# Relative-shift transfers of an attention kernel: residual rows 36 partitions apart, 44 transfers a group in place of 32

## The reference, cut to what matters

```python
AC = einsum('bhid,bhjd->bhij', q + u_bias, k)
BD = einsum('bhid,hjd->bhij', q + v_bias, rp)     # rp: one row for each of 2L-1 distances
BD = _rel_shift(BD)                               # row i is moved left by an amount that depends on i
attn = softmax((AC + BD) * scale)
out = einsum('bhij,bhjd->bhid', attn, v)
```

## Time and profile before

| | |
|---|---|
| time, median of 3 runs | 3833.55 us (3824.93 to 3842.62) |
| time of the profiled execution | 3816.15 us |
| span of that execution | 3814.3 us |
| PE busy | 3139.2 us, 82% |
| ACT busy | 2553.6 us, 67% |
| DVE busy | 2489.7 us, 65% |
| POOL busy | 2399.5 us, 63% |
| granted clock of PE | 0.899 of full speed |

### The profile page before, as it was taken

The page is one execution under the profiler, slowest core; times in us unless marked ns, Lnnn a source line. Parts: engine busy times, 40 slices in busy tenths (PEclk is TensorE's granted clock), DMA queues, the critical chain, the costliest instruction groups (busy, mean ns, idle before and its releaser), DMA issues. The chain is left out here.

```text
span 3814.3 us, 115093 instructions
## 1 busy us (share of the span) xinstructions
PE 3139.2 (82%) x40768; PEld 2161.6 (57%) x40768; DVE 2489.7 (65%) x4784; ACT 2553.6 (67%) x3598; POOL 2399.5 (63%) x4232
## 2 busy tenths in 40 slices
PE   4564588889989888988888887888898989889955
PEld 2443266566656566655666665666665666656644
DVE  1544277677767666776767676776676767667845
ACT  2342477777777777776777776777777777777731
POOL 3234577677767666776777676766777667777700
PEclk7787599999999999998999998999999999999977
DMA  8224899898989898888898998988998888999731
GB/s 235 94 87 141 162 197 196 185 188 195 201 186 199 186 190 190 199 189 175 193 193 197 188 195 175 196 192 190 197 199 194 189 191 203 194 182 200 187 118 44
DMA packets 473330, 688.07 MB, mean 180 GB/s; under 512 B 296752, under 2 KB 394928, under 8 KB 404144
## 3 DMA queue, kind: packets, MB, share of 16 engines
q0 software_dynamic: 327680, 537.92, 66.0%
q1 hardware_dynamic: 145072, 142.63, 15.0%
HBM read 90.06 MB, written 52.43 MB: 37 GB/s over the span
## 5 line engine op out<-in xcount | busy, mean ns | idle before, releaser
L630 POOL DMA_DIRECT2D score<-to_move x4096 | 2267.9, 562 | 987.2 <-issue 500.0
L868 ACT COPY to_move<-pos_bank 128x512 f32<-128x512 f32 x2048 | 1108.6, 594 | 660.6 <-PE pos_bank L736 361.6
L928 DVE CUSTOM_DVE_ANT_0 score<-ac_bank,score 128x1024 f32<-128x1024 f32 x512 | 627.1, 1225 | 908.4 <-PE ac_bank L791 875.9
L805 PEld LDWEIGHTS pt_bank<-ident_sb,score 128*128 128x128 f32 x8192 | 1011.8, 146 | 261.6 <-issue 78.2
L805 PE MATMUL pt_bank<-ident_sb,score 128*128 128x128 f32 x8192 | 1121.8, 282 | 39.9 <-issue 31.7
L880 ACT ACTIVATE score<-score,low 128x2048 f32<-128x2048 f32 x512 | 1032.4, 2016 | 33.6 <-issue 23.6
L937 DVE COPY prob_t<-pt_bank 128x512 f32<-128x512 f32 x1536 | 1009.0, 684 | 15.8 <-PE pt_bank L805 15.2
L736 PE MATMUL pos_bank<-pos,qv 96*32 96x512 bf16 (+15 forms) x12160 | 739.2, 327 | 287.8 <-ACT to_move L868 199.9
L928 DVE CUSTOM_DVE_ANT_0 score<-ac_bank,score,low 128x1024 f32<-128x1024 f32 x512 | 656.5, 1282 | 115.0 <-PE ac_bank L791 102.1
L822 PE MATMUL acc_bank<-prob_t,vs 128*32 128x128 f32 x16384 | 692.3, 287 | 20.3 <-issue 20.1
L791 PE MATMUL ac_bank<-ks,qu 96*128 96x512 bf16 x2048 | 650.9, 401 | 27.8 <-issue 17.1
(11 more groups left out here) (94 smaller groups left out, 962.4 us busy)
## 6 DMA issues: line engine op xcount, KB each, us to landing
score<-to_move POOLq DMA_DIRECT2D x4096, 128.0 KB, 6.0
pos<-pos_parts SPq DMA_DIRECT2D x192, 128.0 KB, 10.2
pos_parts<-part SPq DMA_DIRECT2D x32, 384.0 KB, 4.2
ks<-k_parts SPq DMA_DIRECT2D x192, 64.0 KB, 4.7
qu<-qu_parts SPq DMA_DIRECT2D x768, 16.0 KB, 7.8
qv<-qv_parts SPq DMA_DIRECT2D x576, 16.5 KB, 5.3
v_heads<-v_sb SPq DMA_DIRECT2D x8, 1024.0 KB, 7.3
vs<-v_heads SPq DMA_DIRECT2D x32, 256.0 KB, 9.5
```

The costliest lines, as they stand in the source:

```text
L630: pool.dma_start(score[s::QUAD, dst:dst + FT, :], to_move[s::QUAD, src:src + FT, QUAD - 1 - s:QUAD - 1 - s + L])\
L805: last = pe.matmul(PT[(k * NK + c) % 3][:, t * P:(t + 1) * P], lhsT=score[:, slot(k), c * BANK + t * P:c * BANK + (t + 1) * P], rhs=ident_ ...
L868: act.copy(to_move[:, k % (SRC * FT), c * BANK:(c + 1) * BANK], ring(k, c)[:, :]).then_inc(pos_out, 1)
L928: dve.tensor_tensor_reduce(cols, AC[:, :], cols, SCALE, low[:, slot(k), h - 1:h] if h else -NEG, ALU.add, ALU.min, low[:, slot(k), h:h + 1 ...
```

## The change

The rows that go in one transfer lie 36 partitions apart. To make that possible, PE shifts block r of a tile (rows 32r to 32r+31) by 4r columns less, so that the left-over shift runs from 0 to 43 and row p of block r has left-over shift 31 - (p mod 32) + 4r. A shift then has one to four rows: 20 shifts have four rows, and 8 each have three, two and one. Each shift is one transfer, so a group has 44 in place of 32, with the same 128 rows in all. POOL issues all of them, in an order written out by hand. The tails have 44 columns for each tile in place of 32. `pos` gets 16 columns of zeros on each side, which POOL sets once (4 memsets, and PE waits for them before its first position matmul), since block r now reads up to 12 columns before the table. The counts that ACT and DVE wait for are 16 x 44 a group in place of 16 x 32.

```diff
             QUAD = 32
-            MWIN = L + QUAD
-            CLUSTER = 4
-            MOVE_ORDER = [CLUSTER * c + i for i in range(CLUSTER) for c in range(QUAD // CLUSTER)]
+            LEAN = 4
+            STRIDE = QUAD + LEAN
+            SHIFTS = QUAD + 3 * LEAN
+            MWIN = L + SHIFTS
+            TAIL = SHIFTS
+            PAD = 16
+            def rows_of(shift):
+                first = [r for r in range(4) if LEAN * r <= shift < QUAD + LEAN * r]
+                at = QUAD - 1 - shift + STRIDE * first[0]
+                return slice(at, at + STRIDE * (len(first) - 1) + 1, STRIDE), len(first)
+            PAIRED = [QUAD - 1 - 4 * c for c in (0, 2, 4)] + [LEAN + 3, QUAD + 2 * LEAN - 1]
+            OTHERS = [QUAD - 1 - 4 * c for c in (1, 3)] + [2 * LEAN + 3, QUAD + LEAN - 1]
+            ENDS = [LEAN - 1, SHIFTS - 1]
+            MOVE_ORDER = [shift - i for i in range(LEAN) for shift in PAIRED + OTHERS + ENDS]
...
-            pos = [s2(f"pos{u}", [STACK, NPOS], BF16) for u in range(2)]
+            pos = [s2(f"pos{u}", [STACK, PAD + NPOS + PAD], BF16) for u in range(2)]
...
+                for u in range(2):
+                    pool.memset(pos[u][:, 0:PAD], 0.0).then_inc(padded, 1)
+                    pool.memset(pos[u][:, PAD + NPOS:], 0.0).then_inc(padded, 1)
...
-                    for s in MOVE_ORDER:
-                        pool.dma_start(score[s::QUAD, dst:dst + FT, :],
-                                       to_move[s::QUAD, src:src + FT, QUAD - 1 - s:QUAD - 1 - s + L])\
+                    for shift in MOVE_ORDER:
+                        rows, _ = rows_of(shift)
+                        pool.dma_start(score[rows, dst:dst + FT, :], to_move[rows, src:src + FT, shift:shift + L])\
                             .then_inc(moved[j % DST], 16)
...
                         moves = P - QUAD - row
-                        split = min(max((i + 1) * P - moves - first, 0), width)
-                        at = (NI - 1 - i) * P + moves + first
+                        at = (NI - 1 - i) * P + moves + first - LEAN * (row // QUAD)
+                        split = min(max(L - at, 0), width)
...
-                        last = quads(ring(k, NK), f * QUAD, step, k - FT + 1 + f, L, QUAD)
+                        last = quads(ring(k, NK), f * TAIL, step, k - FT + 1 + f, L, TAIL)
...
+                pe.wait_ge(padded, 4)
```

More of the change, by code:

```diff
@@ L525, in build_program @@
             QUAD = 32
-            MWIN = L + QUAD
-            CLUSTER = 4
-            MOVE_ORDER = [CLUSTER * c + i for i in range(CLUSTER) for c in range(QUAD // CLUSTER)]
+            LEAN = 4
[12 more added lines that the diff above has]
+            MOVE_ORDER = [shift - i for i in range(LEAN) for shift in PAIRED + OTHERS + ENDS]
+            assert sorted(MOVE_ORDER) == list(range(SHIFTS))
             FT = 4
@@ L566, in build_program @@
             moved = [sem(f"moved{i}") for i in range(DST)]
+            padded = sem("padded")
             pos_full, pos_out = sem("pos_full"), sem("pos_out")
@@ L573, in build_program @@
             NLOAD = 16 * len(Q_PARTS)
+            MOVES = 16 * len(MOVE_ORDER)
             def tile_steps(eng, body, past):
@@ L642, in _, with load_stacked @@
             def _(sp):
-                def load_stacked(dst, src, order, hd, lo, n, loaded):
+                def load_stacked(dst, src, order, hd, lo, n, loaded, at=0):
                     for i, part in enumerate(order):
-                        sp.dma_start(dst[i * DH:(i + 1) * DH, 0:n],
+                        sp.dma_start(dst[i * DH:(i + 1) * DH, at:at + n],
                                      src[part, bass.ds(hd * DH, DH), lo:lo + n]).then_inc(loaded, 16)
@@ L661, in load_pos @@
                 def load_pos(step, h):
-                    load_stacked(pos[h % 2], pos_parts, K_PARTS, head(step, h), 0, NPOS, pos_loaded[h % 2])
+                    load_stacked(pos[h % 2], pos_parts, K_PARTS, head(step, h), 0, NPOS, pos_loaded[h % 2], PAD)
                 def load_vs(step, h):
@@ L737, in quads @@
                                                  lhsT=qv[k // FT % 2][:, q0:q0 + QUAD],
-                                                 rhs=pos[u][:, at + lo:at + hi], start=True, stop=True)
+                                                 rhs=pos[u][:, PAD + at + lo:PAD + at + hi], start=True, stop=True)
                     return last
@@ L865, in take @@
                     if c == 0 and k % FT == 0 and group_there(step, j - SRC):
-                        act.wait_ge(moved[(j - SRC) % DST], use_of_dst(step, j - SRC) * (16 * QUAD) + 16 * QUAD)
+                        act.wait_ge(moved[(j - SRC) % DST], use_of_dst(step, j - SRC) * MOVES + MOVES)
                     act.wait_ge(pos_full, group(step, j) * ITEMS + (k % FT * NK + c + 1))
@@ L874, in take_tails @@
                     act.copy(to_move[:, j % SRC * FT:j % SRC * FT + FT, L:MWIN],
-                             ring(k, NK)[:, 0:FT * QUAD].rearrange("p (f w) -> p f w", w=QUAD)).then_inc(pos_out, 1)
+                             ring(k, NK)[:, 0:FT * TAIL].rearrange("p (f w) -> p f w", w=TAIL)).then_inc(pos_out, 1)
                 def exponential(step, k):
@@ L922, in add @@
                     if h == 0 and k % FT == 0:
-                        dve.wait_ge(moved[k // FT % DST], use_of_dst(step, k // FT) * (16 * QUAD) + 16 * QUAD)
+                        dve.wait_ge(moved[k // FT % DST], use_of_dst(step, k // FT) * MOVES + MOVES)
                     if h:
```

## The result

The changed kernel takes 4030.27 us (median of 4), the kernel before 3830.11 us on the same chip: ratio 1.0517, interval 1.0487 to 1.0546. It is 200 us slower, where I had forecast 64 us faster and a range up to 3930. Ratios here compare executions in the faster of two states that every kernel runs in; two of e8's four executions, its profiled one among them, were in the slower, about 1% longer.

What follows compares the result with a forecast made beforehand. A two-group loop through ACT, POOL and the transfer queues was taken as the bound: 20.9 + 1.5 + 23.7 + 3.0 = 49.1 us, 24.65 a group with 0.1 added, against 25.18; so 3833.55 - 64 = 3770 us, range 3570 to 3930.

Steps and rivals of the forecast that it cites:

- four parts: Loop over two groups before: copies to tails 21.1 us, tails to issue 1.5, issue 17.7, last issue to next copy 9.7.
- What bounds the kernel now: Attention stage: a two-group loop through ACT, POOL and the queues sets the 25.18 us period; POOL idles a third.
- the last part of the loop: From POOL's last issue to ACT's next first copy: 9.7 us before, forecast about 3.0.
- Part 1: Spacing of a transfer's rows: 8 KB in 0.42 us in place of 0.61, so queues no longer pile up.
- Part 2: Twelve more issues on POOL: 44 take 23.7 us a group, midway between cost by packets and flat cost.
- the sum by packets: POOL's issue cost following packets, 76, 72 and 68 in place of 80: 23.0 us for 44 issues.
- The upper bound of 24.3: POOL's 44 issues at a flat 0.553 us each.
- The row of SP in the earlier trace: SP issued 256 KB and 16 KB in 0.43 us each, read as a flat issue cost.
- Part 3: Wait between tails and POOL's issue, 1.5 us: vanishes when the tails have long been there.
- Parts 4 and 5: Wider tails: 0.07 us in two groups, 4 us over the span; memsets, PE's new wait and larger counts: nothing.
- the first part of the loop: From ACT's first copy to the end of the tails: mean 21.1 us before, 20.9 forecast.
- POOL becomes the bound, slower: Rival: 44 flat-cost issues take 24.3 us, plus 1.5 between groups, period 25.8, 3913 us; chance 0.25.

Runs made afterwards that it cites:

- e8: Changed kernel with its 44 transfers in plain order of the shift: 5748.77 us, ratio 1.4908.
- e9: Kernel before with 12 idle memsets on POOL between the 32 issues of a group: 3997.78 us, ratio 1.0437.
- e13: Kernel before with 18 idle memsets on POOL among the 32 issues of a group: 4131.62 us, ratio 1.0827.
- e14: Kernel before with its 32 four-row transfers respaced to rows 36 or 4 apart, plus 18 idle memsets a group on POOL: 4006.55 us, ratio 1.0489.
- e7: Changed kernel without the loads of the position table after the first two heads: 3898.35 us, ratio 1.0200.
- e5: Changed kernel with the 8 single-row transfers of a group issued by SP, 36 left on POOL: 3980.70 us, ratio 1.0400.
- e6: Changed kernel with the 8 single-row and 8 two-row transfers of a group issued by SP, 28 left on POOL: 5003.02 us, ratio 1.3045.
- e4: Kernel before with the loads of a head's position table four bodies later: 4065.70 us, ratio 1.0602.
- e10: Kernel before with the six loads of a position table issued one a body over six bodies: 3930.98 us, ratio 1.0235.
- e16: Changed kernel, position loads spread, SP issuing the 8 single rows between its query loads for position and content products: 4009.45 us, ratio 1.0423.
- e17: Changed kernel, position loads spread, SP issuing only 4 single rows between its position and content query loads, 40 transfers on POOL: 4208.76 us, ratio 1.0983.
- e2: Kernel before with its 32 four-row transfers made of rows 36 or 4 apart, same issue count and bytes: 3672.67 us, ratio 0.9576.
- e12: Changed kernel, position loads spread, SP issuing the 8 single rows one body later, after its query loads: 3913.25 us, ratio 1.0222.

## Why the prediction was wrong

The loop was the right frame: its four parts add up to the period in every run. Three of its terms were mis-sized.

- *What bounds the kernel now.* Right. e9, e13 and e14 show that time added to POOL, which idled a third of the time, appears in the period.
- *Part 1, "nothing piles up, and the last part of the loop falls from 9.7 to about 3.0 us".* This step failed: 6.12 measured, 3.1 us over in a loop of two groups. Its base was 0.42 us for a run of 8 KB, taken from loads that span 128 partitions; it was 0.571. Spacing makes a transfer with nothing before it fast: in the packet records, the first four runs of a group whose predecessor had wholly landed take 645 ns in the median before (45 groups of 12 to 117) and 381 after (30). Over the whole stream it does much less, 0.573 to 0.517 us in the mean, since transfers in flight meet each other (e8) and SP's loads. Of the 3.1 us over, 2.3 go with the position loads (e7: without them the last part is 3.80); the prediction had only "somewhat more" for all of SP's loads.
- *Part 2, 44 issues in 23.7 us.* 24.8 measured, 1.1 over. The cost is nearly flat (541 ns with one row, 570 with four), where the sum by packets had 0.47 us for one row. Its 76, 72 and 68 packets were wrong too: by the counts of the changed kernel, e5 and e6 it is 80 for three or two rows and 32 for one. The upper bound of 24.3 was itself short by 0.5, since the first two issues of each eleven take longer (634 and 599 ns) and a pause of 0.2 lies before the last four of a group. The row of SP in the earlier trace rows had pointed the right way, and I took the middle.
- *Part 3, the wait vanishes when POOL is late.* Right in kind (0.19 us after its last issue), wrong in use: I kept 1.5 as a mean and added 0.1 a group for hindering each other. The tails of every second group wait 3.5 us, mostly for POOL; the mean is 2.15, 0.65 over.
- *Parts 4 and 5.* Right: the copy of the tails went from 0.27 to 0.30 us, the first part of the loop didn't grow.

Together 3.1 + 1.1 + 0.65, 0.1 of the copies, less the 0.2 added = 4.75 us for two groups; 54.04 - 49.3 = 4.74. The first term alone doesn't explain the loss: with the last part at 3.0 the period would be (54.04 - 3.12) / 2 = 25.5, still not under the 25.3 of the kernel before. The other base was off too: five loops gave 9.7 for the last part before, all of groups 12 to 117 give 10.38.

The rival "POOL becomes the bound, slower" came nearest, but by another way: POOL alone would give 25.8 us by its sum, and 24.79 + 0.19 = 25.0 as measured, and the period was 27.0. What I wrote as the reason for a small gain, that 12 issues nearly eat what the queues give back, was the reason for the loss: 7.1 against 4.3.

Open: why e4 and e10 cost the kernel before 6% and 2.4%; why POOL's own transfers land late in e16 and e17, and why e17 is the worse; what divides the rest of the last part between transfers meeting each other and other loads.

## What to carry to other kernels

When a change makes each transfer faster but needs more of them, ask first whether issue time is in the loop that sets the period, even if the issuing engine idles a third of the time; idle work put on that engine prices it in one run. A pace read from one kind of transfer holds only for what is in flight beside it: order and partners can matter more than the shape. Leave the other transfers' place in time alone, or measure it, since this schedule lost 6% by moving one table's loads four bodies.

## What the runs showed of the hardware

- A transfer issued by POOL takes it about 0.55 us whether it has four, three, two or one row (sixteen runs of 8 KB to four): medians 570, 553, 547 and 541 ns, all 5632 issues from 536 to 792.
- The order of the same 5632 transfers moves the ratio from 1.05 to 1.49, and the median landing from 4.0 to 18.3 us.
- With nothing of the group before in flight, the first four runs of 8 KB of a group take 645 ns in the median with rows 32 apart and 379 to 381 with spread rows (e2, changed kernel); in the stream the means are 0.573, 0.496 (e2) and 0.517 us.
- On SP an issue of a transfer of one or two rows takes 1.0 to 1.1 us in the mean in e5, e6, e12, e16 and e17 (17.05 us for 16 in e6, but 4.90 for 8 in the lines of e12), up to twice POOL's, where SP's single loads at the start took 0.43.
